# A fused embedding, state-space and attention kernel: the attention stage's small products and transposes on 128 rows and 128 columns

## The reference

```
xn = layernorm(h)                                  # 64 channels
q, k, v = xn @ W (4 heads x 4 experts x 16; 4 x 16; 4 x 16)
p = softmax(q k^T, masked)    per head and expert;  o = p v
mix = experts gated per head + residual
fx = layernorm(mix);  f1 = relu(fx @ fc1 + b1);  f2 = f1 @ fc2 + b2
out = h + gated, normed heads of (f2 + fx)
```

## Time and profile before

| | |
|---|---|
| three runs | 1568.27, 1572.8, 1576.63 us; median 1572.8 |
| profiled execution | 1554.56 us, span from first to last instruction 1552.8 us |
| mean granted TensorE clock in it | 0.895 |
| PE matmul busy | 1260.9 us, 81% of the span, 11,006 records |
| PE weight load busy | 607.0 us, 39% |
| ACT, DVE, POOL busy | 834.1, 827.8, 424.4 us |

### The profile page before, as it was taken

The page is one execution under the profiler, slowest core; times in us unless marked ns, Lnnn a source line. Parts: engine busy times, 40 slices in busy tenths (PEclk is TensorE's granted clock), DMA queues, the critical chain, the costliest instruction groups (busy, mean ns, idle before and its releaser), DMA issues.

```text
span 1552.8 us, 28784 instructions
## 1 busy us (share of the span) xinstructions
PE 1260.9 (81%) x11006; PEld 607.0 (39%) x11103; DVE 827.8 (53%) x1683; ACT 834.1 (54%) x1050; POOL 424.4 (27%) x621
## 2 busy tenths in 40 slices
PE   4896378851589988998999899899899989988942
PEld 3363276730235333433433334343443334333311
DVE  4745863276744634565365465548345544743443
ACT  0231134530256875676477567668746864875810
POOL 2000130037132214323132432432413232242421
PEclk9897689985589999999799999999987997999965
DMA  8999199503390082045008305502800550180000
GB/s 152 182 188 172 35 184 202 107 16 84 78 119 1 13 156 39 12 102 100 1 12 154 48 13 108 94 1 75 139 1 13 118 84 1 60 132 15 1 15 9
DMA packets 122173, 117.99 MB, mean 76 GB/s; under 512 B 74621, under 2 KB 91276, under 8 KB 121882
## 3 DMA queue, kind: packets, MB, share of 16 engines
q1 hardware_dynamic: 117988, 115.60, 39.6%
q10 hardware_dynamic: 3733, 0.60, 0.3%
q0 software_dynamic: 320, 0.04, 0.0%
HBM read 88.36 MB, written 22.95 MB: 72 GB/s over the span
## 4 chain that ended last, share of the span: by engine, by line
PE 41%; DVE 9%; ACT 7%; issue 5%; DMA 5%; POOL 5%; SPq 3%; POOLq 0%; DVEq 0%; ACTq 0%
PE b_pso L1969 14%; PE b_pss L1945 11%; ACT b_pb L2080 6%; POOL b_stat L2105 3%; PE b_psm L1996 3%; PE b_psm L2013 3%; DMA qk_parts_b<-b_qs 3%; PE b_psm L2027 3%; DMA b_qop<-bound_part 2%; PE b_psm L1928 2%; POOL b_pb L2124 2%; PE b_psm L2008 2%; PE b_psm L2005 2%; PE b_psm L2032 1%; SPq L1881 1%
## 5 line engine op out<-in xcount | busy, mean ns | idle before, releaser
L2080 ACT ACTIVATE b_pb<-b_pss 128x1024 f32<-128x1024 f32 (+2 forms) x736 | 663.2, 935 | 329.5 <-PE b_pss L1945 242.9
L2124 POOL TENSOR_SCALAR_AFFINE_SELECT b_pb<-b_pb 128x256 f32<-128x256 f32 (+1 forms) x544 | 225.0, 432 | 711.4 <-ACT b_pb L2080 703.7
L1969 PE MATMUL b_pso<-b_pb,b_vop 128*32 128x77 f32 (+4 forms) x5376 | 383.0, 393 | 35.8 <-POOL b_pb L2124 33.5
L1945 PE MATMUL b_pss<-b_qop,b_kop 128*128 128x512 bf16 (+3 forms) x1439 | 330.4, 336 | 29.0 <-issue 10.7
L1945 PEld LDWEIGHTS b_pss<-b_qop,b_kop 128*128 128x128 bf16 x1536 | 119.9, 102 | 237.6 <-ACT b_pb L2080 139.1
L1969 PEld LDWEIGHTS b_pso<-b_pb,b_vop 128*32 128x32 f32 x5376 | 116.4, 112 | 216.5 <-issue 163.6
L2309 DVE TENSOR_TENSOR b_ofm<-b_pso,b_mk 128x512 f32<-128x512 f32 (+1 forms) x96 | 51.7, 538 | 142.6 <-PE b_pso L1969 141.6
L2105 POOL TENSOR_TENSOR b_stat<-b_stat,b_mh 128x18 f32<-128x18 f32 x34 | 108.8, 3219 | 38.8 <-DVE b_stat L2381 27.3
L915 PE MATMUL psc<-tz,ub 128*64 128x128 f32 x1152 | 80.0, 283 | 44.5 <-DVE tz L1036 35.6
L2191 DVE COPY b_ot<-b_psm 128x336 f32<-128x336 f32 (+1 forms) x96 | 40.1, 418 | 118.0 <-PE b_psm L1996 117.7
L1996 PEld LDWEIGHTS b_psm<-w_mixer,b_ofm 128*128 128x128 f32 (+1 forms) x576 | 72.3, 194 | 60.7 <-issue 39.4
(11 more groups left out here) (383 smaller groups left out, 1534.9 us busy)
## 6 DMA issues: line engine op xcount, KB each, us to landing
b_qop<-qk_parts_b SPq DMA_DIRECT2D x192, 144.0 KB
tz<-taps SPq DMA_DIRECT2D x64, 304.0 KB, 9.6
x<-in_x SPq DMA_DIRECT2D x16, 1024.0 KB, 13.1
qk_parts_b<-b_qs SPq DMA_DIRECT2D x16, 864.0 KB, 5.0
b_kop<-qk_parts_b SPq DMA_DIRECT2D x192, 36.0 KB
b_mk<-b_mskf SPq DMA_DIRECT2D x128, 36.0 KB, 4.3
qk_parts_b<-b_ks SPq DMA_DIRECT2D x8, 432.0 KB, 3.9
n_late<-id_d SPq DMA_DIRECT2D x1, 2400.0 KB, 9.4
```

The source lines that it names most:

```text
L1945: mm = pe.matmul(pss[:, u % 2, b, col:col + w], lhs, qop[:, n, e, q0:q0 + w], start=True, stop=True, skip_group_check=True)
L1969: mm = pe.matmul(pso[VW * ee:VW * (ee + 1), (3 * n + x) % 2, q0 - QT * x:q0 - QT * x + w], vop[0:r, j, n, :], pb[0:r, slot_, b, cc:cc + w] ...
L2080: nc.scalar.activation(pb[:, s % PB, 0:nb, 0:w], pss[:, s % 2, 0:nb, 0:w], ACT.Exp, scale=float(HD) ** 0.5).then_inc(exped, 1)
L2124: ins = pool.affine_select(out=v_, in_=v_, compare_op=ALU.is_ge, fill=0.0, base=0, pattern=pat, channel_multiplier=-1)
```

## The change

All small jobs but oturn are given 128 rows and 128 columns. `xt`, `fxt`, `hx1`, `pm`, `wall`, `backm` and `fcw` get 128 partitions, `fcw`, `blkqb` and `blkkb` 128 columns; what is added holds zeros. seen reads the columns 384 to 511 of `wall`, a feature of the keys the columns 256 to 383 (with the value weights, whose output is ignored). A transpose takes two neighbouring position tiles as its 128 columns, and only the first 64 output rows are read; the ninth has no neighbour and stays at 64. knorm keeps its 64 rows of squares. The numbers of matmuls, their moving columns, the order of the jobs and the instructions that empty the banks stay as they are. New are eight memsets: four on DVE in the front stage, one on DVE and three on POOL at the start of the attention stage, where the chain of `late_ok` grows from 7 to 10.

```diff
-        self.blkqb = sb("w_blkqb", [P, 2, HE], BF16)
-        self.blkkb = sb("w_blkkb", [D, HE], BF16)
+        self.blkqb = sb("w_blkqb", [P, 2, P], BF16)
+        self.blkkb = sb("w_blkkb", [D, P], BF16)
...
-        self.wall = sb("w_all", [D + 1, 512])
-        self.fcw = sb("w_fcw", [D + 1, 2, D])
+        self.wall = sb("w_all", [P, 512])
+        self.fcw = sb("w_fcw", [P, 2, P])
...
-        self.backm = sb("w_backm", [D, BACKW])
+        self.backm = sb("w_backm", [P, BACKW])
...
                 ch.done(nc.vector.memset(wblk[:], 0.0))
+                ch.done(nc.vector.memset(w.wall[:], 0.0))
+                ch.done(nc.vector.memset(w.backm[D:P], 0.0))
+                ch.done(nc.vector.memset(w.blkqb[:], 0.0))
+                ch.done(nc.vector.memset(w.blkkb[:], 0.0))
...
-        xt = sb("b_xt", [D + 1, LP])
+        xt = sb("b_xt", [P, LP])
...
-        fxt = sb("b_fxt", [D + 1, LP])
-        hx1 = sb("b_hx1", [D + 1, LP])
-        pm = sb("b_pm", [D, LP])
+        fxt = sb("b_fxt", [P, LP])
+        hx1 = sb("b_hx1", [P, LP])
+        pm = sb("b_pm", [P, LP])
...
-                                sp.wait_ge(late_ok, 7)
+                                sp.wait_ge(late_ok, 10)
...
                     for a in range(*c):
-                        mm = pe.transpose(bank()[0:D, (a - c[0]) * P:(a - c[0] + 1) * P], src[:, a, :], ident[:])
+                        m = min(2, NA - a)
+                        mm = pe.transpose(bank()[0:D * m, (a - c[0]) * P:(a - c[0] + 1) * P], src[:, a:a + m, :].rearrange("p a d -> p (a d)"), ident[:])
...
-                        mm = pe.matmul(bank()[0:D, 0:FB], wall[:, 384:448], xt[:, c * FB:(c + 1) * FB], start=True, stop=True)
+                        mm = pe.matmul(bank()[:, 0:FB], wall[:, 384:512], xt[:, c * FB:(c + 1) * FB], start=True, stop=True)
...
-                        m = P if g < 2 else D
                         gate(base)
-                        mm = pe.matmul(bank()[0:m, 0:FB], wall[:, g * P:g * P + m], xt[:, x * FB:(x + 1) * FB], start=True, stop=True)
+                        mm = pe.matmul(bank()[:, 0:FB], wall[:, g * P:g * P + P], xt[:, x * FB:(x + 1) * FB], start=True, stop=True)
...
-                        mm = pe.matmul(bank()[0:HE, 0:FB], blkkb[:], squares[0:D, slot[2, c], :], start=True, stop=True)
+                        mm = pe.matmul(bank()[:, 0:FB], blkkb[:], squares[0:D, slot[2, c], :], start=True, stop=True)
...
-                        pe.matmul(bank()[0:HE, 0:FB], blkqb[:, 0, :], squares[:, slot[0, c], :], start=True, stop=False)
-                        mm = pe.matmul(bank()[0:HE, 0:FB], blkqb[:, 1, :], squares[:, slot[1, c], :], start=False, stop=True)
+                        pe.matmul(bank()[:, 0:FB], blkqb[:, 0, :], squares[:, slot[0, c], :], start=True, stop=False)
+                        mm = pe.matmul(bank()[:, 0:FB], blkqb[:, 1, :], squares[:, slot[1, c], :], start=False, stop=True)
...
-                        mm = pe.matmul(bank()[0:D, 0:FB], fcw[:, i, :], (hx1 if i else fxt)[:, c * FB:(c + 1) * FB], start=True, stop=True)
+                        mm = pe.matmul(bank()[:, 0:FB], fcw[:, i, :], (hx1 if i else fxt)[:, c * FB:(c + 1) * FB], start=True, stop=True)
...
-                        pe.wait_ge(late_ok, 7)
+                        pe.wait_ge(late_ok, 10)
...
                         pool.wait_ge(late_ok, 4)
+                        pool.memset(fxt[D:P], 0.0).then_inc(late_ok, 1)
+                        pool.wait_ge(late_ok, 5)
                         pool.memset(fxt[D:D + 1], 1.0).then_inc(late_ok, 1)
-                        pool.wait_ge(late_ok, 5)
+                        pool.wait_ge(late_ok, 6)
+                        pool.memset(hx1[D:P], 0.0).then_inc(late_ok, 1)
+                        pool.wait_ge(late_ok, 7)
                         pool.memset(hx1[D:D + 1], 1.0).then_inc(late_ok, 1)
-                        pool.wait_ge(late_ok, 6)
+                        pool.wait_ge(late_ok, 8)
+                        pool.memset(pm[D:P], 0.0).then_inc(late_ok, 1)
+                        pool.wait_ge(late_ok, 9)
                         pool.memset(ot[:], 1.0).then_inc(late_ok, 1)
...
                 ch = Chain(v, dve)
+                ch.step(nc.vector.memset(xt[D:P], 0.0))
                 ch.done(nc.vector.memset(xt[D:D + 1], 1.0))
```

More of the change, by code:

```diff
@@ L280, in layer_weights @@
                     sp.dma_start(w.center[:], t["c_center"]).then_inc(weights, 16)
-                    sp.dma_start(w.backm[:, 0:D], t["c_center"]).then_inc(weights, 16)
+                    sp.dma_start(w.backm[0:D, 0:D], t["c_center"]).then_inc(weights, 16)
                 def mixer_weights():
@@ L1041, in _ @@
                 cp(wb[D:P, 1], psw[D:P, 0:D]).then_inc(psw_out, 1)
-                ch.done(cp(w.blkqb[:], w.blkq[:]))
-                ch.done(cp(w.blkkb[:], w.blkk[:]))
+                ch.done(cp(w.blkqb[:, :, 0:HE], w.blkq[:]))
+                ch.done(cp(w.blkkb[:, 0:HE], w.blkk[:]))
                 for n in range(NH):
@@ L1050, in _ @@
                 v.wait_ge(wt, 2)
-                cp(w.wall[:], psf[0:D + 1, 0, :]).then_inc(psw_out, 1)
+                cp(w.wall[0:D + 1], psf[0:D + 1, 0, :]).then_inc(psw_out, 1)
                 ch.step(nc.vector.memset(w.ones[:], 0.0))
@@ L1054, in _ @@
                 v.wait_ge(wt, 3)
-                cp(w.backm[:, D:], psf[0:D, 1, 0:NH * NH]).then_inc(psw_out, 1)
+                cp(w.backm[0:D, D:], psf[0:D, 1, 0:NH * NH]).then_inc(psw_out, 1)
                 v.wait_ge(ul_ok, 1)
@@ L2234, in empty @@
                             v.wait_ge(free, base + k[0] + 2)
-                            ch.step(ts(pm[:], fxt[0:D], 0.0, None, ALU.not_equal))
-                        give(stt(hx1[0:D, s_], bank()[0:D, 0:FB], 0.0, pm[:, s_], ALU.max, ALU.mult))
+                            ch.step(ts(pm[0:D], fxt[0:D], 0.0, None, ALU.not_equal))
+                        give(stt(hx1[0:D, s_], bank()[0:D, 0:FB], 0.0, pm[0:D, s_], ALU.max, ALU.mult))
                     elif kind == "fc2":
                         s_ = slice(c * FB, (c + 1) * FB)
-                        ch.step(tt(pm[:, s_], bank()[0:D, 0:FB], pm[:, s_], ALU.mult))
-                        give(tt(pm[:, s_], pm[:, s_], fxt[0:D, s_], ALU.add))
+                        ch.step(tt(pm[0:D, s_], bank()[0:D, 0:FB], pm[0:D, s_], ALU.mult))
+                        give(tt(pm[0:D, s_], pm[0:D, s_], fxt[0:D, s_], ALU.add))
                     else:
```

## The result

The changed kernel takes 1525.91 us (median of 4 runs, 1522.55 to 1528.47), the kernel before beside it 1570.53 us (4 runs, 1561.62 to 1576.63): a ratio of 0.9719, 95% interval 0.9665 to 0.9773. It is faster by 2.8%, where 3.8% was forecast. The median lies inside the stated range, 1500 to 1562 us, and 0.9 us above the narrower 1500 to 1525 that stood for "all falls gone". The profiled execution takes 1524.09 us with a span of 1522.4 us and a mean granted clock of 0.918, against 1554.6, 1552.8 and 0.895.

What follows compares the result with a forecast made beforehand. The prediction took PE to bound the kernel, with TensorE's clock making like batches differ. From 1554.6 us it took off 30.1 for clock falls and 11 for stops, with 0 for memsets: 1513.5 us, range 1500 to 1562.

Steps and rivals of the forecast that it cites:

- all falls gone: The main forecast: every clock fall behind tok disappears, own range 1500 to 1525 us, chance 0.66.
- The bound: In the attention batches PE is the bound, busy 119 of 129.9 us; like batches differ by TensorE's clock.
- The clock term: Clock falls behind the thin back and tok jobs in four like batches go once shapes are full: 30.1 us saved.
- the sign: What would show it right: all six like batches at 127 to 129 us, clock 0.98 or more, no fall at tok.
- the stops' term: PE's stops around narrow products in the attention batches go: 11 us saved, bounds 0 to 17.
- the 3.4 us falls: Short low-clock stretches following a PE wait at the change of batch, 3.4 us each; said to stay.
- I take 1.6: Of 2.1 us of stops saved per batch, 1.6 was kept, the rest given back where PE waits for DVE or POOL.
- The memsets: Added memsets in the front stage and at the attention stage's start cost nothing; without cover, 5 us.
- The sum: 1554.6 - 30.1 - 11 + 0 = 1513.5 us; the same 1513 expected for the median, 3.8% below 1572.8.
- (a): Rival: the clock stays as it is and only the stops go, 1544 us profiled, 1562 by the median; chance 0.13.
- (b): Rival: the falls become fewer or shorter, not none, about half of 30 us staying, 1528 to 1540 us; chance 0.13.
- (c): Rival: slower, with a long fall in each of the seven batches with a tok, 1587 us; chance 0.05.

Runs made afterwards that it cites:

- e3: Changed kernel with back on 64 rows and tok on 65 again, everything else on 128 rows and columns: 1547.08 us, ratio 0.9876.
- e7: Changed kernel with only tok on 65 rows again: 1533.16 us, ratio 0.9805.
- e11: Changed kernel with ones in place of zeros in the unused rows of the four data tiles, weights' rows still zero: 1520.93 us, ratio 0.9712.
- e1: Changed kernel with the added rows kept and the added columns taken back (64 or 16, transposes 64): 1529.58 us, ratio 0.9801.
- e2: Changed kernel with the added columns kept and the added rows not used (back 64 rows, the other products 65): 1562.34 us, ratio 0.998.
- experiment 6: Traced PE's wait for the queries, then tried four versions of the changed kernel with earlier query features, three with later mixing parts: 1507.09 to 1542.58 us.
- e12: e10 with the added columns taken back and the rows kept: 1513.41 us, ratio 0.9717.
- e10: Changed kernel with the last three query-feature jobs one or two steps earlier and DVE's mixing parts moved to steps 76 to 82: 1507.09 us, ratio 0.9622.
- e8: Changed kernel with all transposes back on 64 columns: 1528.83 us, ratio 0.9768.
- e6: Changed kernel with only back on 64 rows again: 1523.0 us, ratio 0.974.

## Why the prediction was right and where it was not

**The bound.** Right: PE, 116 to 120 us of each batch, and the like batches of before differed by the clock.

**The clock term, 30.1 us.** Right in mechanism and size. Falls behind tok: four before (23.9, 23.9, 17.1 and 3.4 us), none after; the like batches lost 30.5 us, and rows alone, with all stops left in, gave 2.0% of the time. The step that I could not settle blind, whether zero rows count, is settled by e3 and e7, where taking the zero rows away brings falls back, and by e11, where ones do no more; that rows and not busy time decide here is settled by the same two beside the changed kernel. The Trainium skill ("TensorE: Matmul & The Clock Gate", What's actually happening) lets the clock follow how busy PE has been. The runs don't agree with busy time alone: with 3.08 us of 3.40 the clock fell on 65 rows in tok and did not on 128, and with 3.19 it fell on thin rows. Of columns the prediction said more than the runs bear out: thin columns were to hold the level down. With full rows, 64 columns bring no fall (e1); with thin rows, 128 columns leave low stretches of 17 to 20 us (e2). What the columns do to the length of a fall was not tried by itself.

Three of the six windows are longer than the 127 to 129 us that were named as the sign, and one reads 0.97 where 0.98 was the least: that is the stops' term, and the 3.4 us falls.

**The 3.4 us falls.** Said to stay; eight before, seven after. The prediction put them at the change of batch. Only one of the eight stands there, behind a wait of 3.1 us for the queries; the other seven begin 28 to 31 us into a batch, behind one wait of 2.0 or 2.1 us for POOL's mask (L2124), with POOL busy for 3.2 to 3.4 of the 3.4 us ahead of the fall; ahead of the one at 863.4 it had spent 6.40 us on statistics (L2105). In the changed kernel four are of that kind, and three begin within 1.0 us of a batch's first exponential, behind waits of 2.4 to 2.6 us for the queries.

**The stops, 11 us: this is the term that was mis-sized.** The stops themselves went as counted, seen from score to score 1.14 us as forecast. But of 2.1 us a batch I said "I take 1.6", and named only waits for DVE and POOL as takers. Counted from a batch's first exponential, the last mixer product starts at 127.0 us in the two batches of before without a fall behind tok, and at 126.1 on the mean of the changed kernel's six: 0.9 us ahead. At the batch's end 0.1 us is left of it. What took it back is PE's wait for the transferred queries, 7.4 us in all before and 12.4 after, which the prediction had no term for. Being early does not explain that wait: the last query norm is 1.0 us earlier too, so a way of the same length would have brought the queries earlier by as much. The way itself grew, by 4.7 us over seven changes (experiment 6). And e1, where PE is no earlier than before (127.3 us at the last mixer product), waits 11.1 us and takes 130.5 us a batch against 129.5. Why the write is at times 1.7 to 2.0 us longer is open, and with it whether the loss belongs to the change or to these executions.

In place of the forecast 11 us the profiled pair shows 0.1 us a batch, 1.1 in the first and 1.0 in the rest, 2 to 3 us in all. Against e1, which has the rows, the stops and nearly as long a wait, the like batches gain 130.5 - 129.4 = 1.1 us each, 6.6 in all, of which one more short fall in e1 is a part. The medians of e1 and the changed kernel differ by 3.7 us, those of e12 and e10 by 6.3, the ratios of e1 and the changed kernel by 13 us with intervals that overlap, those of e12 and e10 by 15; and columns without rows (e2) gave 3 us by the ratio, not told from none. So the columns' worth lies between 2 and 15 us, and these runs don't narrow it further. e10 shows that the wait costs what it takes: starting the last query features one to two steps earlier, with the mixing parts moved, gave 1.4 us a batch. That these are the microseconds that the stops had saved is not shown; e12 was meant to show it and is inconclusive.

The Trainium skill ("TensorEngine Tiling (Array Packing)", Key Properties) says that a change of tiling mode drains TensorE. For products the runs agree, 0.54 and 0.80 us in e1 against 0.44 and 0.70. At the 128x64 transposes no stop shows: e8 has none either, and its time can't be told from the changed kernel's. Whether the mode changes there at all, no trace says.

**The memsets, 0.** Right. The changed kernel's DVE timeline at the start of the stage:

```profile
371.11 1.02 DVE L2177 MEMSET b_xt<- 64x1152 f32 x1 [4.82 <-PEq L885]
...
375.61 3.19 DVE L2358 TENSOR_SCALAR b_statx<-b_statx 128x9 f32<-128x9 f32 x1
```

and POOL's:

```profile
393.46 1.15 POOL L2149 MEMSET b_fxt<- 64x1152 f32 x1
...
436.80 0.97 POOL L2128 TENSOR_SCALAR_AFFINE_SELECT b_pb<-b_pb 128x256 f32<-128x256 f32 x2 [34.87 <-ACT b_pb L2084]
```

The lines are those foreseen in the earlier trace rows: 1.02 us on DVE under a wait that was there, three of 1.15 on POOL with 34.9 us of idle time left behind them.

**The sum.** In the profiled pair the forecast was 10.6 us too low (1513.5 against 1524.1): 8 to 9 from the stops, 2.2 from scatter ahead of the first exponential. For the median it was 12.4 too low. The forecast put the 18 us between the median and the profiled execution of before down to more batches with a long fall, which would go too. The changed kernel's four runs lie within 6 us, around the profiled one, and the kernel before's within 15. That agrees, but no unprofiled run has a trace, so it stays argued.

**The rivals.** (a), zeros don't count, falls with the changed kernel and e1 beside e3, and with e11. (b), half the falls stay, falls: no long one stayed; but e6 and e7 show how near it lay, one thin job brings some back. (c), more falls than before, has its nearest case in e2, wide columns without the rows: five long falls in six batches and no gain. Its mechanism, a lower busy share ahead of the fall, is not what e2 shows, though: PE is busy 3.09 of 3.30 us there against 3.19 of 3.40 before, the same share, and five against four may be chance.

## What to carry to other kernels

Where like stretches of work differ in time, order them by granted clock first, and look at the shapes of the matmuls in front of each fall, not only at PE's gaps: filling thin operands up to 128 rows cost nothing here and gave 2.0%. A gain inside a period counts only as far as the slowest way into the next period has slack, so name that way (here queries through DRAM), measure its pieces at each change, and start it earlier. Then look at what the move pushes into: by the ratios the last triple one to two steps earlier, with DVE's mixing parts out of the way, gave 15 us more, and the query features up to three steps earlier, with the mixing parts left where they were, lost 26.

## What the runs showed of the hardware that was not expected

- The clock depended on the number of rows in use at equal or smaller PE busy time, and on how many of two neighbouring jobs were thin: both, six of six batches (e3); back alone, two (e6); tok alone, one (e7, at 3.08 us busy of 3.40 as in the changed kernel); none, none of 54. Rows of zeros counted as rows of ones (e11). Lower busy time still brought a fall on full rows (e12, 2.39 of 3.40 us).
- Wide columns without the rows did not hold the clock up: five falls of 17 to 20 us in e2, where before there were four, of 3.4 to 24.
- A change of the array's columns from 128 to 64 and back stopped PE for about 0.1 us each way at f32 products (0.54 and 0.80 against 0.44 and 0.70 us), but not at the f32 transposes recorded as 128x64 (0.44 us from scores to transpose, narrow or wide).
- A DVE instruction on 128x9 elements took 3.19 us and ended at 378.80 us, where a memset of POOL that had begun at 370.99 and took 7.77 us ended at 378.76. Before it took 3.56 us and ended at 375.48, and POOL's memset ended at 375.44. Instruction and memset ended together both times; that the one held the other is argued, no run separates them.
- The write of the last queries to DRAM took 5.6 us at some changes of batch and up to 7.6 at others. In the change at 952.8 31 of its 32 landings came by 938.77 us and the last at 940.77, and the reads waited for it.
